# Edge attention of the first graph layer: the running maximum over spans of sixteen slots instead of groups of eight, a ring of 24 gathered rows, and six throwaway products per span

## The reference, cut to what matters

```python
q = (x @ Wq + bq).reshape(n, HEADS, DIM_OUT)
k = (x @ Wk + bk).reshape(n, HEADS, DIM_OUT)
v = (x @ Wv + bv).reshape(n, HEADS, DIM_OUT)
scores = jnp.einsum('ehd,ehd->eh', q[src], k[dst]) / jnp.sqrt(32)
m = jax.ops.segment_max(scores, dst, num_segments=n)
e = jnp.exp(scores - m[dst])
z = jax.ops.segment_sum(e, dst, num_segments=n)
out = jax.ops.segment_sum(v[src] * (e / z[dst])[:, :, None], dst, num_segments=n)
```

## Time and profile before

| what | before |
|---|---|
| median of 3 runs | 7604.67 us (7602.22 to 7616.29) |
| the profiled execution | 7620.67 us |
| its span, first to last instruction | 7618.7 us, 77,992 instructions |
| mean granted TensorE clock | 0.81 |
| PE / DVE / ACT / POOL busy, share of the span | 80% / 64% / 20% / 60% |
| the stage that is changed | gathers from 335.72 us on, last sums added at 1884.0 us |

### The profile page before, as it was taken

How to read it: one execution, slowest core, us unless ns; L and a number is a source line. 1 busy time by engine, 2 the same in 40 slices (tenths; PEclk the granted TensorE clock), 3 DMA queues, 4 the chain that set the end, 5 groups by cost and what they waited for, 6 DMA issues and landing times. The chain is left out here.

```text
span 7618.7 us, 77992 instructions
## 1 busy us (share of the span) xinstructions
PE 6110.5 (80%) x22430; PEld 3541.0 (46%) x22430; DVE 4883.7 (64%) x10533; ACT 1507.6 (20%) x3148; POOL 4547.8 (60%) x4618
## 2 busy tenths in 40 slices
PE   8699999998368777788888799978888857777773
PEld 4366666665233333344444344433333335555552
DVE  7799988998757666544444344444444467777767
ACT  5222222222100000000000155500000033333321
POOL 1155555554477777777777511177777727777750
PEclk9799999999675655689988799955555579898886
DMA  2266666666433333544444544433333454445553
GB/s 92 71 178 176 176 175 177 176 176 159 143 101 96 99 98 98 108 132 132 133 131 129 123 166 163 158 107 101 102 101 101 99 150 132 130 134 132 133 102 102
DMA packets 429281, 989.50 MB, mean 130 GB/s; under 512 B 119363, under 2 KB 202497, under 8 KB 422214
## 3 DMA queue, kind: packets, MB, share of 16 engines
q0 software_dynamic: 242400, 709.04, 35.4%
q1 hardware_dynamic: 186470, 275.48, 11.0%
HBM read 851.94 MB, written 132.00 MB: 129 GB/s over the span
## 5 line engine op out<-in xcount | busy, mean ns | idle before, releaser
L876 PE MATMUL psum<-rows,oh 128*128 128x257 f32 (+1 forms) x5280 | 2440.2, 577 | 649.3 <-DMA rows<-h_tab,src_i 190.5
L876 PEld LDWEIGHTS psum<-rows,oh 128*128 128x128 f32 x5280 | 1174.9, 264 | 1866.9 <-issue 1072.4
L885 DVE TENSOR_TENSOR acc<-acc,psum 128x257 f32 (+1 forms) x1760 | 741.6, 421 | 1110.2 <-PE psum L876 986.8
L799 POOL DMA_INDIRECT rows<-qv_tab,src_i x880 | 848.4, 964 | 848.6 <-PE psum L1060 498.0
L818 POOL DMA_INDIRECT rows<-h_tab,src_i x880 | 906.6, 1030 | 291.0 <-issue 241.7
L818 POOL DMA_INDIRECT rows<-hw_tab,rel_i x880 | 874.3, 994 | 283.9 <-issue 267.9
L818 POOL DMA_INDIRECT rows<-h_tab,wts x880 | 873.1, 992 | 268.2 <-issue 252.4
L885 DVE TENSOR_TENSOR kh<-kh,psum 128x257 f32 x880 | 371.0, 422 | 636.5 <-PE psum L876 597.4
L1400 POOL DMA_INDIRECT kh<-xh_tab,src_i x576 | 577.3, 1002 | 175.6 <-issue 123.7
L1668 DVE TENSOR_TENSOR acc<-acc,psum 128x272 f32 x880 | 378.5, 430 | 242.9 <-PE psum L1486 215.6
L1009 PE MATMUL psum<-kh,oht 128*128 x1760 | 510.6, 403 | 5.6
(11 more groups left out here) (468 smaller groups left out, 9297.2 us busy)
## 6 DMA issues: line engine op xcount, KB each, us to landing
wts<-node_rows SPq DMA_DIRECT2D x220, 256.0 KB
hw_tab<-acc SPq DMA_DIRECT2D x50, 1024.0 KB, 4.1
rows<-part_tab SPq DMA_DIRECT2D x50, 512.0 KB, 5.4
rows<-qv_tab,src_i POOLq DMA_INDIRECT x880, 3.6
rows<-h_tab,src_i POOLq DMA_INDIRECT x880, 2.8
rows<-h_tab,wts POOLq DMA_INDIRECT x880, 2.8
rows<-hw_tab,rel_i POOLq DMA_INDIRECT x880, 2.8
qv_tab<-rows SPq DMA_DIRECT2D x50, 260.0 KB, 2.0
```

The source lines that it names most:

```text
L799: nc.gpsimd.indirect_dma_start(rows[:, b, 0:width], None, table, bass.IndirectOffsetOnAxis(index, 0)).then_inc(ring[b], 16)
L876: mm = nc.tensor.matmul(slot_bank(n, plan), oh[:, n % RING // GROUP, n % GROUP], row, start=True, stop=True)
L885: nc.vector.tensor_tensor(to, to, slot_bank(n, plan), ALU.add).then_inc(acc_done, 1)
```

## The change

`dot_attention()` treats spans of 16 slots (`SPAN = 2 * GROUP`) in the place of groups of 8. Per span there is one transposition of 128 rows of scores to both directions (one product with the 256 columns of `both_ways`), two scans of 128 rows in `scan_within`, one row of ends of 256, one `join_slots`, one `scan_across`, one pair of `differences`, one `lower_sums`, and two ACT exponentials of half a span each. The sums over heads stay at eight slots an instruction, multiplications and weighings at two. The lists of all engines are written anew. The throwaway products stand once in a span.

The gathered rows get a third place for eight slots: `thirds` adds `big`, a tensor that holds what were `dl`, `last`, `parts` and `wts`. `dl` and `last` are stored to HBM at the start of the stage and loaded again in the next one. The gather of slot n+24 now waits for the sum of slot n. Small one-row tiles move to `shared`. The rest of the diff renumbers semaphore counts in the later stages.

```diff
+    dl_tab, last_tab = dram("dl_tab", [P, SLOTS]), dram("last_tab", [P, SLOTS])
...
+    big = sb("big", [P, BEFORE_WTS + 22 * D])
+    dl, last = big[:, 0:SLOTS], big[:, SLOTS:2 * SLOTS]
...
+        SPAN = 2 * GROUP
+        thirds = [rows[:, k * GROUP:(k + 1) * GROUP, :] for k in range(2)]
+        thirds += [big[:, 0:GROUP * ROW].rearrange("p (s w) -> p s w", w=ROW)]
...
         def on_gpsimd(pool):
+            for n in range(SLOTS):
+                if n == RING:
+                    pool.wait_ge(flags_out, KEPT)
+                if n >= HELD:
+                    pool.wait_ge(agg_done, summed(n - HELD))
...
         def on_sync(sp):
+            for to, of in ((dl_tab, dl), (last_tab, last)):
+                sp.dma_start(to, of).then_inc(flags_out, 16)
...
+        def turn_hot(pe, g):
+            pe.wait_ge(far_ready, nth(g))
+            pe.wait_ge(wide_ready, g)
+            if g >= 2:
+                pe.wait_ge(weight_ready, weights_in(g // 2 - 1, 1))
...
+        def turn_scores(pe, t):
+            pe.wait_ge(score_ready, done(t))
+            nc.tensor.matmul(psum[:, 4, 0:2 * P], score[t % 2], both_ways, start=True, stop=True).then_inc(score_ps, 1)
...
+        def differences(pe, t):
+            pe.wait_ge(across_ready, nth(t))
+            pe.wait_ge(alpha_ready, done(t))
+            nc.tensor.matmul(ps_diff, ident[:, :], score[t % 2], start=True, stop=False)
+            nc.tensor.matmul(ps_diff, across[t % 2], negated, start=False, stop=True).then_inc(diff_ps, 1)
...
         def on_tensor(pe):
...
+            for t in spans:
+                more, later = t + 1 in spans, t + 2 in spans
+                if more:
+                    keys_of(pe, t + 1, 2, places)
+                sums_of(pe, t, range(0, 2))
+                if more:
+                    keys_of(pe, t + 1, 3, places)
+                sums_of(pe, t, range(2, 5))
+                if more:
+                    turn_hot(pe, 2 * t + 2)
+                    places = places_of(t + 1, 1)
+                sums_of(pe, t, range(5, 8))
+                if more:
+                    keys_of(pe, t + 1, 4, places)
+                    keys_of(pe, t + 1, 5, places)
+                sums_of(pe, t, range(8, 9))
+                if more:
+                    turn_hot(pe, 2 * t + 3)
+                sums_of(pe, t, range(9, 10))
+                if more:
+                    keys_of(pe, t + 1, 6, places)
+                sums_of(pe, t, range(10, 11))
+                if more:
+                    keys_of(pe, t + 1, 7, places)
...
+                sums_of(pe, t, range(11, 12))
+                if more:
+                    keep_busy(pe, t + 1, 7, 6)
+                    turn_scores(pe, t + 1)
+                sums_of(pe, t, range(12, 13))
+                if later:
+                    keys_of(pe, t + 2, 0, places)
+                if more:
+                    row_of_ends(pe, t + 1)
+                sums_of(pe, t, range(13, 14))
+                if more:
+                    spread_bounds(pe, t + 1)
+                    fall_of_node(pe, t + 1)
+                sums_of(pe, t, range(14, 15))
+                if later:
+                    keys_of(pe, t + 2, 1, places)
+                if more:
+                    differences(pe, t + 1)
+                sums_of(pe, t, range(15, 16))
...
         def on_vector(dve):
...
+            for t in spans:
...
+                lower_sums(dve, c, t, places[0])
+                weigh_values(dve, t, 0)
+                if more:
+                    multiply_keys(dve, t + 1, 2)
+                add(dve, t, 0, places)
+                weigh_values(dve, t, 1)
+                if more:
+                    multiply_keys(dve, t + 1, 3)
+                add(dve, t, 1, places)
+                add(dve, t, 2, places)
+                weigh_values(dve, t, 2)
+                add(dve, t, 3, places)
+                if more:
+                    sum_scores(dve, t + 1, 0)
+                add(dve, t, 4, places)
+                weigh_values(dve, t, 3)
+                for s in range(5, 8):
+                    add(dve, t, s, places)
+                weigh_values(dve, t, 4)
+                places = places_at(t, 1)
+                if more:
+                    multiply_keys(dve, t + 1, 4)
+                add(dve, t, 8, places)
+                if more:
+                    multiply_keys(dve, t + 1, 5)
+                weigh_values(dve, t, 5)
+                add(dve, t, 9, places)
+                if more:
+                    multiply_keys(dve, t + 1, 6)
+                add(dve, t, 10, places)
+                if more:
+                    multiply_keys(dve, t + 1, 7)
+                add(dve, t, 11, places)
+                if more:
+                    sum_scores(dve, t + 1, 1)
+                weigh_values(dve, t, 6)
+                if more:
+                    scan_within(dve, t + 1)
+                add(dve, t, 12, places)
+                weigh_values(dve, t, 7)
+                if more:
+                    join_slots(dve, c, t + 1)
+                add(dve, t, 13, places)
+                if later:
+                    multiply_keys(dve, t + 2, 0)
+                if more:
+                    scan_across(dve, c, t + 1)
+                add(dve, t, 14, places)
+                if later:
+                    multiply_keys(dve, t + 2, 1)
+                add(dve, t, 15, places)
```

More of the change, by code:

```diff
@@ L963, in group_rows, with by_slot_head @@
[L963 to L967, removed]
+        def by_slot_head(ap):
+            return ap.rearrange("p (h s) -> p s h", s=SPAN)
         CLEARED = 20 * SUMW
         def on_gpsimd(pool):
[L972 to L977, removed]
@@ L1046, in fall_of_node @@
[L1046 to L1054, removed]
+        def fall_of_node(pe, t):
+            node = hot[2 * t % len(hot)][0:1, 0]
+            nc.tensor.matmul(ps_fall, node, by_link(bound[t % 2])[:, :, 0], start=True, stop=False)
+            nc.tensor.matmul(ps_fall, node, inherited[t % 2], start=False, stop=True).then_inc(fall_ps, 1)
@@ L1056, in sums_of @@
                 if s % 2 == 0:
[L1057 to L1061, removed]
+                    pe.wait_ge(msg_ready, pair(t, s // 2))
+                pe.wait_ge(acc_done, summed(n - len(banks)))
@@ L1063, in on_tensor @@
+                nc.tensor.matmul(psum[:, banks[n % len(banks)], 0:ACCW], hot[n // GROUP % len(hot)][:, s % GROUP],
+                                 row_of(n)[:, vat:vat + ACCW], start=True, stop=True).then_inc(agg_done, 1)
         def on_tensor(pe):
             pe.wait_ge(begun, 1)
[L1065 to L1074, removed]
-            fall_of_node(pe, 0, 0)
-            keys_of(pe, 0, 1, 1, places)
-            differences(pe, 0, 0)
-            for g, (j, h) in enumerate(groups):
-                more, later = at(g + 1), at(g + 2)
+            turn_hot(pe, 0)
+            turn_hot(pe, 1)
+            for half in range(2):
+                places = places_of(0, half)
+                for q in range(4 * half, 4 * half + 4):
+                    keys_of(pe, 0, q, places)
@@ L1270, in on_vector @@
+            join_slots(dve, c, 0)
+            scan_across(dve, c, 0)
+            multiply_keys(dve, 1, 0)
+            multiply_keys(dve, 1, 1)
             dve.wait_ge(sums_clear, 1)
             c.wait()
-            places = acc_places(slot(0, 0), GROUP)
-            for g, (j, h) in enumerate(groups):
-                more, later = at(g + 1), at(g + 2)
-                lower_sums(dve, c, j, h, places[0])
+            places = places_at(0, 0)
+            for t in spans:
+                more, later = t + 1 in spans, t + 2 in spans
+                lower_sums(dve, c, t, places[0])
+                weigh_values(dve, t, 0)
@@ L1803, in l0e_sync @@
         load(1)
+        for to, of in ((dl, dl_tab), (last, last_tab)):
+            sp.dma_start(to, of).then_inc(flags_out, 16)
         for t in range(TILES):
```

489 lines of the change are left out of this document (242 added, 247 removed).

## The result

The changed kernel takes 7742.94 us (median of 4 runs, 7730.03 to 7757.86) where the kernel before, timed beside it, takes 7605.98 (7602.22 to 7616.29): 1.0179 times as long, 95% interval 1.0156 to 1.0201, or 137 us more. The prediction said 7608 and gave 7565 to 7692; the measured time lies 51 us above that range.

The account below looks back on a forecast made before the run. VectorE was taken to set the pace, with stops where TensorE answers late. Stage: -4.6 us from the walk, +8 for the clock, about 3.5 us later; 7608 us against the median of 7604.67, range 7565 to 7692.

Parts of the forecast that it names:

- the walk: Stage's new order stepped through: 27.5 us a span against 27.66 for two groups before, stage 1543.7 us at unchanged clock.
- The clock: TensorE's granted clock in the stage: falls cost between 0 and 82 us, 8 us taken.
- a fall in six spans or so: TensorE's clock falls in one span of about six, behind idle stretches, about 1.5 us each, 8 us in all.
- idle ahead of sums 4 and 6: In each span TensorE stands idle 1.6 us before sum 4 and 2.0 us before sum 6.
- the bound of 82 us: Upper bound of the clock's cost over the stage, with one fall in every span.
- The rule cited: TensorE's throttled state is the default and activity lifts it; halving the throwaways therefore speaks against the change; no size given.
- the rival of a fall in every span: Clock falls in the 6.6 us TensorE block every span: +82 us on the stage, 7682 us; chance 0.25.
- Work and stops: VectorE per span: 22.84 us of work and 4.67 us of stops, against 24.50 and 3.16 for two groups before.
- Beginning and end: Stage's ends: 42.3 us from first gather to first lowering, and 16.4 us for the last span.
- The copies of `dl` and `last`: Stores at the stage's start and loads in the next stage: 0 us taken, at most 10.
- The ring of 24: Rival: last slots' gathers have 3 us; 7627 us if landing takes 4.1 us, some 7700 at 5.5; chance 0.11.
- The faster rival: VectorE's work sets the pace, stops stay 3.16 us: 26.0 us a span, about 7525 us; chance 0.24 with all between.

Follow-up runs that it names:

- e5_products_moved: Changed kernel with three key pairs moved on TensorE into its idle stretches, no product added or taken away; 7637.44 us.
- e7_both_orders: e5_products_moved with key pair 0 of the next span also moved earlier, and VectorE's weighings 3 and 4 earlier; 7606.91 us, 1.0013 of the kernel before.
- e9_late_multiplications: e7_both_orders with multiplications 3 and 7 and addition 11 later on VectorE, sums 10 and 11 ahead of pair 7 on TensorE; 7576.52 us, 0.9962 of before.

## Why the prediction was wrong

Against the walk the stage came out 118 us longer than the 1551.7 that were forecast (1543.7 and 8). By its terms:

- **The clock, +89 us.** The step that failed is "I take a fall in six spans or so, 8 us, since TensorE's work over a whole span is nearer to the stage of before than to the last attention". It measured 97 us: 63 falls in 54 spans. The mechanism and the first place were right (idle ahead of sums 4 and 6, forecast 1.6 and 2.0 us, the latter 1.81 here, a fall in the block of key products behind), but the frequency was mis-sized: 22 falls there, not six. The other 40 come behind a second place, which was left out, and so even the bound of 82 us, one fall in every span, was too low. The walk has the scores, the row of ends and the bounds go to TensorE and back, and prices VectorE's stops there, but never lists TensorE's own idle time in that chain: 1.06 and 1.10 us with little between. The work over a whole span was the wrong measure; e5_products_moved keeps exactly that work and holds the clock by its order alone.
- **The rule cited.** The Trainium skill (TensorE: Matmul & The Clock Gate, What's actually happening) has activity lift a clock that is otherwise throttled. The runs agree: products without a reader added, 109 us less time (7742.94 to 7633.69; against the kernel before timed beside each, 137 us over becomes 36); taken out, 183 us more in the kernel before (7778.66, one execution, against 7595.25). The prediction weighed it as speaking against the change, and gave the rival of a fall in every span 0.25.
- **Work and stops, +22 us.** VectorE's work of 22.84 us was right by the durations. An undisturbed span was forecast at 27.5 and takes 27.90 on average, 27.69 in the one shown. Its stops are where the walk put them: ahead of addition 6 (0.46, forecast 0.64), addition 8 (0.45, 0.55), multiplication 3 (0.32, 0.47) and multiplication 7 (0.46, 0.52). The one ahead of multiplication 3 is put down to TensorE's product and not to the gather.
- **Beginning and end, +3 and +4 us.** From the first gather to the first lowering it takes 45.3 us, not 42.3: two multiplications of the next span wait 1.96 and 1.87 us for their products there. The last span takes 20.7, not 16.4, with waits of up to 1.34 for sums.
- **The copies of `dl` and `last`**, taken as 0 to 10 us: the 7 us outside the stage would hold them, but were not told apart from scatter between executions.
- **The ring of 24** (0.11) was not the cause of this result, with 14.6 us of waits for rows. With the clock held, rows that land late are the next limit, 56 to 61 us in 43 or 44 spans. Whether a longer ring, the pace at which GpSimd issues (one gather every 1.26 us where nothing holds it) or the transfers beside the gathers would mend that was not told apart.
- **The faster rival** (VectorE's work sets the pace, 7525) was not reached by any order: at a held clock and with the best order found, 26.74 us a span leave 3.9 us of stops over the 22.84 of work.

## What to carry to other kernels

Moving work so that one engine saves time also moves the holes of the others: list TensorE's idle stretches in the new order, each with what it does just ahead and behind, before pricing anything at the upper clock, and take a fall at every such place as the bound, not a mean over the loop (here 22 and 40 of 54 spans fell). If a change that removes work comes out slower, read the granted clock by short stretches first; a filled hole or a product pulled ahead into it is a cheap test. When the clock is mended, look at when each load lands and when it is wanted, since the next limit may be a load that now has too little time.

## What was not expected of the hardware

- The longest wait does not tell whether the clock falls. In e7_both_orders TensorE waits 1.3 us for a weighing in nearly every span and stands at 1.00; the changed kernel falls behind a wait of 1.10 us. The waits add up to some 270 us in e5_products_moved as in the changed kernel (600 to 1800 us), with four falls in the stage there and 63 here. And two spans with the same waits, shown above, differ in it. Which products around a wait hold the clock was narrowed to two places, not measured one by one.
- In the kernel before, without its six products, TensorE's clock falls in 58 of 109 groups, which costs 183 us, with a longest wait of 1.7 us for the scores.
- A median over all gathers hides the one that matters. From issue to landing it is 3.8 us after, in e5_products_moved and in e9_late_multiplications (3.6 before), but the gather of slot 15 takes 4.0, 4.9 and 4.6 us, and there VectorE waits.
